# Experts by token: indirect transfers to seats of 128 rows in place of all experts on all tokens

## The chip, the cores and the metric

The kernel runs on one core of a Trainium2 chip. The metric is the device time of one execution in microseconds. The profile comes from one profiled execution; its span runs from the first to the last instruction.

## The reference

One transformer layer on x of 2048 tokens by 256, in fp32. First attention with 16 heads of 128 and weights given as codes and scales, then a mixture of eight experts of which each token uses two:

```python
x = x + layernorm(attention(layernorm(x)))
z = layernorm(x)
probs = softmax(z @ Wr)                      # 8 experts
topk_w, topk_idx = top_k(probs, 2)
topk_w = topk_w / topk_w.sum(-1)
combine = (topk_w * one_hot(topk_idx, 8)).sum(k)
h = silu(z @ Wg[e]) * (z @ Wu[e])            # every e: 256 -> 176
out = sum_e combine[:, e] * (h @ Wd[e])      # 176 -> 256
x = x + layernorm(out)
```

## The kernel before, in words

Five engines run programs written by hand, in written order, and hand over through semaphores: SyncE (`block.sync`) issues all DMAs, GpSimd (`block.gpsimd`), TensorE (`block.tensor`), ScalarE (`block.scalar`), VectorE (`block.vector`). For precision every factor of a product is split in a high and a low part (`_hi`, `_lo`, fp32r), and `product3` (L497 to L499) makes three matmuls of each product.

Attention runs over 128 blocks (16 heads by 8 blocks of 256 rows). SyncE's loop `for n in range(HALVES)` (L318) issues some weight loads of the next head and then `turn_blocks(n)` (L307), 16 transfers of 128 KB that turn the probabilities (L316); it waits first until GpSimd's `pT_lo` (L409) has freed the buffer (L193). The change leaves this part as it is but for what it adds to SyncE's loop and ahead of GpSimd's.

The expert stage begins once `acc` holds the sum over the heads. `pre(c, s)` handles a chunk of 512 tokens in eleven small steps: first normalization of `acc` (L1002), residual on GpSimd (L466), moments (L989), second normalization, transposes (L686) to `xT_hi` (L934) and `xT_lo`, logits for the eight experts (sixteen matmuls of 16 and 8 columns, L696 and L699), exponentials, rank (L1253 to L1264), and `comb`, the two weights of each token, transposed and split. `PRE_AT` (L236) says in which step each part stands.

The matmuls run in 44 steps, 4 chunks by 11 groups of 128 of the 1408 hidden columns of all eight experts. A step makes gate and up (`gate_up`, 12 matmuls of 512 columns into `ps_s`), spreads the tokens' weights over the hidden columns with one matmul (`expand_comb`, L735), takes silu on ScalarE (L961), two products on VectorE (L1312, L1316), the split (L967 on ScalarE, L478 on GpSimd), and `down` two steps later (12 matmuls of 256 columns, L749 to L752), which sums all experts in `ps_a`. So every token goes through all eight experts, and a weight of zero takes six of them out. The splits of the weights (`split_hi` L918 and L923, `split_lo`) stand between the steps of the first chunk. `hooks` puts the next chunk's `pre` and the last chunk's `post` (moments, normalization, residual L473, store) between the steps, so three of the four chunks are routed beside matmuls.

```python
for n in range(STEPS + LAG):
    if n < STEPS:
        gate_up(n)
        expand_comb(n)
    if n >= LAG:
        down(n - LAG)
    hooks(n, pre, post)
```

## Time and profile before

| | us |
|---|---|
| median of 3 runs | 2115.59 (2112.35 to 2116.29) |
| span of the profiled execution | 2115.3 |
| TensorE busy in the span | 2049.6 (97%), 13236 matmuls |
| VectorE, ScalarE, GpSimd busy | 1730.4, 1410.8, 1548.8 |
| mean granted TensorE clock | 0.986 |

The page gives no total of its own for the profiled execution beside its span; the median of the runs is 0.3 us above the span. Matmuls are pipelined and a busy TensorE counts their overlap once, so the distance between two starts is what a matmul costs, and its own duration is longer. A granted clock of 1.00 is 2.4 GHz and 0.50 is 1.2 GHz.

### The profile page before, as it was taken

Reading aid. Unit: us, or ns where it says so; the run is one execution under the profiler, and the core shown is the slowest. Engines: PE = TensorE matmul, PEld = TensorE weight load, DVE = VectorE, ACT = ScalarE, POOL = GpSimd, SP = SyncE. Lnnn points to the kernel's source line nnn. Section 1 sums busy time; section 2 is a strip of 40 time slices with the busy share of each in tenths; the row PEclk is TensorE's granted clock in tenths of the full one; section 3 lists DMA queues with packets and bytes.
Section 4 is the critical chain, followed back from the end, with each engine's and each line's share of the span. In section 5 each row is a group of like instructions: output and inputs, shape, how many; then the busy total and the mean of one; then the engine's idle time right before and its main releaser. Section 6 shows DMA issues by size and latency. Waiting matters only on the chain.

```text
span 2115.3 us, 36713 instructions
## 1 busy us (share of the span) xinstructions
PE 2049.6 (97%) x13236; PEld 1866.8 (88%) x13236; DVE 1730.4 (82%) x2523; ACT 1410.8 (67%) x2575; POOL 1548.8 (73%) x1329
## 2 busy tenths in 40 slices
PE   7999999999999999999999999999999999949998
PEld 5899999999999999999999999899989999838887
DVE  6888878988989888988888898888888888865553
ACT  5777767776777667776677677766777677625343
POOL 2679778886879777877797787877787678846333
PEclk9999999999999999999999999999999999969999
DMA  4667657776667666766676666766676567740000
GB/s 99 155 156 178 158 139 163 170 164 158 146 160 175 151 149 153 181 155 140 162 174 161 148 155 155 179 147 150 153 170 154 136 161 165 161 121 1 11 11 21
DMA packets 216599, 298.50 MB, mean 141 GB/s; under 512 B 44897, under 2 KB 85345, under 8 KB 216417
## 3 DMA queue, kind: packets, MB, share of 16 engines
q1 hardware_dynamic: 216416, 296.15, 59.8%
q8 instruction: 105, 1.72, 0.4%
q14 instruction: 78, 0.63, 0.1%
HBM read 25.46 MB, written 2.10 MB: 13 GB/s over the span
## 4 chain that ended last, share of the span: by engine, by line
PE 84%; SPq 5%; POOL 3%; DVE 3%; ACT 2%; DMA 1%; issue 1%; POOLq 0%; DVEq 0%; ACTq 0%
PE ps_s L497 14%; PE ps_s L498 14%; PE ps_s L499 14%; PE ps_a L499 12%; PE ps_a L498 12%; PE ps_a L497 12%; SPq L316 4%; POOL pT_lo L409 3%; ACT probs L819 1%; PE ps_a L749 1%; PE ps_a L752 1%; PE ps_a L751 1%; DMA pT<-probs 1%; DVE part_max L1065 1%; PE ps_s L735 0%
## 5 line engine op out<-in xcount | busy, mean ns | idle before, releaser
L409 POOL TENSOR_TENSOR pT_lo<-pT,pT_hi 128x512 fp32r<-128x512 f32 x1024 | 1302.8, 1302 | 358.6 <-ACT pT_hi L832 357.6
L832 ACT ACTIVATE pT_hi<-pT 128x512 fp32r<-128x512 f32 x1024 | 612.4, 628 | 232.6 <-DMA pT<-probs 163.5
L819 ACT ACTIVATE probs<-ps_s,shift 128x1024 f32<-128x1024 f32 x512 | 566.6, 1109 | 223.3 <-DVE shift L1074 223.0
L1065 DVE TENSOR_REDUCE part_max<-ps_s 128x1 f32<-128x1024 f32 x512 | 622.0, 1217 | 67.5 <-PE ps_s L499 65.8
L1084 DVE STREAM_TRANSPOSE probs<-probs 128x1024 f32<-128x1024 f32 x512 | 619.4, 1229 | 65.4 <-ACT probs L819 64.6
L497 PE MATMUL ps_a<-pT_hi,v_hi 128*128 128x256 f32 x2048 | 578.7, 283 | 1.5 <-POOL pT_lo L409 1.4
L499 PE MATMUL ps_a<-pT_hi,v_lo 128*128 128x256 f32 x2048 | 579.9, 283 | 0.0
L498 PE MATMUL ps_a<-pT_lo,v_hi 128*128 128x256 f32 x2048 | 579.7, 283 | 0.0
L497 PE MATMUL ps_s<-kT_hi,qT_hi 128*128 128x512 f32 x1024 | 405.2, 396 | 11.7 <-ACT probs L819 8.5
L497 PEld LDWEIGHTS ps_a<-pT_hi,v_hi 128*128 128x128 f32 x2048 | 391.8, 191 | 19.0 <-POOL pT_lo L409 2.5
L498 PEld LDWEIGHTS ps_a<-pT_lo,v_hi 128*128 128x128 f32 x2048 | 391.8, 191 | 15.5
L498 PE MATMUL ps_s<-kT_lo,qT_hi 128*128 128x512 f32 x1024 | 403.9, 394 | 0.0
L499 PE MATMUL ps_s<-kT_hi,qT_lo 128*128 128x512 f32 x1024 | 399.2, 390 | 0.0
L499 PEld LDWEIGHTS ps_a<-pT_hi,v_lo 128*128 128x128 f32 x2048 | 391.8, 191 | 0.0
L499 PEld LDWEIGHTS ps_s<-kT_hi,qT_lo 128*128 128x128 f32 x1024 | 192.4, 188 | 43.7
L497 PEld LDWEIGHTS ps_s<-kT_hi,qT_hi 128*128 128x128 f32 x1024 | 193.9, 189 | 39.4 <-ACT probs L819 10.4
L498 PEld LDWEIGHTS ps_s<-kT_lo,qT_hi 128*128 128x128 f32 x1024 | 193.8, 189 | 21.5
L478 POOL TENSOR_TENSOR h_lo<-hid,h_hi 128x512 fp32r<-128x512 f32 x44 | 57.0, 1295 | 100.3 <-ACT h_hi L967 100.1
L1127 DVE SCALAR_TENSOR_TENSOR acc<-ps_a,rinv,acc 128x256 f32<-128x256 f32 x240 | 104.1, 475 | 6.1 <-PE ps_a L499 5.9
L819 ACT ACTIVATION_READ_ACCUMULATOR probs<-ps_s,shift 128x1 f32 x512 | 99.0, 193 | 0.0
L1312 DVE TENSOR_TENSOR hid<-silu_g,ps_s 128x512 f32<-128x512 f32 x44 | 30.2, 687 | 77.4 <-PE ps_s L499 68.0
L961 ACT ACTIVATE silu_g<-ps_s 128x512 f32<-128x512 f32 x44 | 26.3, 599 | 89.5 <-PE ps_s L499 89.4
(160 smaller groups left out, 2917.5 us busy)
## 6 DMA issues: line engine op xcount, KB each, us to landing
pT<-probs SPq DMA_DIRECT2D x2048, 128.0 KB, 2.5
pT<-in_L_attn_x SPq DMA_DIRECT2D x4, 512.0 KB, 5.7
codes<-in_L_attn_wk_codes SPq DMA_DIRECT2D x16, 128.0 KB, 2.4
scales<-in_L_attn_wk_scales SPq DMA_DIRECT2D x64, 32.0 KB, 3.0
codes<-in_L_attn_wo_codes SPq DMA_DIRECT2D x16, 128.0 KB, 2.3
scales<-in_L_attn_wo_scales SPq DMA_DIRECT2D x64, 32.0 KB, 1.9
x<-in_L_attn_x SPq DMA_DIRECT2D x4, 512.0 KB, 7.1
layer_out<-x SPq DMA_DIRECT2D x8, 256.0 KB, 2.1
```

Source lines behind the costliest of these rows:

```text
L316: sp.dma_start(dst, src[:, :, b, :]).then_inc(pT_loaded[s % 2], 16)
L409: pool.tensor_tensor(pT_lo[:, p, :].rearrange("p (i n) -> p i n", i=Q4), pT[:, s % 2, g, :, t:t + 2, :].rearrange("p i t q -> p i (t q)"), ...
L478: pool.tensor_tensor(h_lo[:, n % HRING, :], hid[:, n % 2, :], full(h_hi[:, n % HRING, :]), ALU.subtract)\
L497: nc.tensor.matmul(dst, lhs_hi, rhs_hi, start=first, stop=False)
L498: nc.tensor.matmul(dst, lhs_hi, rhs_lo, start=False, stop=False)
L499: return nc.tensor.matmul(dst, lhs_lo, rhs_hi, start=False, stop=last)
L819: nc.scalar.activation(out, src, ACT.Exp, bias=shift[:, s % SLOTS, r:r + 1], scale=SCALE, accum_out=sums[:, s % SLOTS, r, g:g + 1])\
L832: nc.scalar.activation(pT_hi[:, p, :].rearrange("p (i n) -> p i n", i=Q4), pT[:, s % 2, g, :, t:t + 2, :].rearrange("p i t q -> p i (t q)" ...
L1065: V.tensor_reduce(part_max[:, s % SLOTS, r, g:g + 1], ring_of("s", w, NG2 * r + g), AX.X, ALU.max)\
L1084: V.transpose(tile, tile).then_inc(sm["p_turned"], 1)
L1127: ins = V.scalar_tensor_tensor(acc[:, t, :], part, scale, acc[:, t, :], ALU.mult, ALU.add)
L1312: V.tensor_tensor(hid[:, n % 2, :], silu_g[:, n % 2, :], ps_bank(b), ALU.mult)\
```

## The change

The 16 tiles of 128 tokens form two parts of eight, routed in three runs (tiles 0 to 3, 4 to 7, 8 to 15). A part has 23 seats of 128 rows, enough for any routing: each expert gets as many whole seats as its tokens need. Matmuls with a triangle of ones and with ones count each token's place, VectorE works out for each token two row numbers and for each seat its expert, and GpSimd sends each tile's normalized rows twice by indirect transfer to `x_rows` in HBM. SyncE loads a seat, TensorE transposes it, reads the seat's expert number into a register and multiplies with that expert's weights alone: the rows are now the stationary operand and the weights, 352 and 256 columns, the moving one. Results are stored to `y_rows`, and GpSimd fetches two rows for each token, which are weighed and added. The rows of `x_rows` are cleared during attention, since a seat may be part empty. All weights are split before the first seat. The three parts of the stage (routing of part 0, of part 1, the seats) stand in written order on each engine. The core of the diff:

```diff
-    G = E * I // P
-    STEPS = NCH * G
+    KD = I // 2
+    RUNS = [(0, 4), (4, 4), (8, 8)]
+    PART_TILES = [(0, 8), (8, 8)]
+    SEATS = [2 * n + E - 1 for _, n in PART_TILES]
+    NS = sum(SEATS)
+    XR = 4
+    GR = 4
+    YS = 4
+    GO = SEATS[0] + 8
 @block.sync
                 turn_blocks(n)
+                if NH <= n < NH + NS:
+                    sp.dma_start(x_rows[u][seat * P:(seat + 1) * P, :], zeros[:, :]).then_inc(x_cleared, 16)
...
+            for n in range(NS + 9):
+                if n < NS:
+                    load_seat(n)
+                if n >= 9:
+                    store_seat(n - 9)
 @block.gpsimd
+            def send(r):
+                if r == 0:
+                    pool.wait_ge(x_cleared, 16 * NS)
+                pool.wait_ge(sm["row_done"], r + 1)
+                for t in tiles_of(r):
+                    pool.wait_ge(sm["xn2_done"], t + 1)
+                    for k in range(2):
+                        pool.indirect_dma_start(x_rows[PART_OF_RUN[r]][:, :], bass.IndirectOffsetOnAxis(row[:, t, k:k + 1], 0),
+                                                acc[:, t, :], None).then_inc(x_sent[PART_OF_RUN[r]], 16)
+            def fetch(t):
+                u = part_of_tile(t)
+                if t == PART_TILES[u][0]:
+                    pool.wait_ge(sm["gu_lo_done"], E)
+                    for b in range(YS):
+                        pool.wait_ge(y_stored[b], 16 * len(range(b, FIRST_SEAT[u] + SEATS[u], YS)))
+                wait(pool, "ysum_done", t - GR + 1)
+                for k in range(2):
+                    pool.indirect_dma_start(yg[:, t % GR, k, :], None, y_rows[u][:, :],
+                                            bass.IndirectOffsetOnAxis(row[:, t, k:k + 1], 0))\
+                        .then_inc(yg_loaded[t % GR], 16)
-            pre_all(pool, pre)
-            prepare_pick()
...
+            residual(0)
+            residual(1)
+            for e in range(E):
+                gate_up_lo(e)
+            send(0)
+            send(1)
+            residual(2)
+            for e in range(E):
+                down_lo(e)
+            send(2)
+            for t in range(PART_TILES[0][1]):
+                fetch(t)
+            for t in range(PART_TILES[0][1]):
+                add_residual(t)
+            for t in range(PART_TILES[0][1], TT):
+                fetch(t)
+            for t in range(PART_TILES[0][1], TT):
+                add_residual(t)
 @block.tensor
+            def gate_up(j):
+                if n == 0:
+                    pe.wait_ge(sm["expert_ready"], u + 1)
+                if j == 0:
+                    pe.wait_ge(sm["gu_lo_done"], E)
+                expert_at[j] = pe.value_load(expert_i[0:1, u, n:n + 1], min_val=0, max_val=E - 1)
+                wait(pe, "xs_lo_done", j + 1)
+                wait(pe, "h_done", j - 1)
+                for c in range(DC):
+                    hi, lo = xs_hi[:, j % 2, c * P:(c + 1) * P], xs_lo[:, j % 2, c * P:(c + 1) * P]
+                    w_h, w_l = (gu_both[:, c, b, bass.ds(expert_at[j], 1), :].rearrange("p a n -> p (a n)")
+                                for b in range(2))
+                    last = product3(ps_gate(j), hi, lo, w_h, w_l, first=c == 0, last=c == DC - 1)
+            def down(j):
+                pe.wait_ge(sm["hs_lo_done"], j + 1)
+                wait(pe, "y_copied", j)
+                for k in range(2):
+                    hi, lo = hs_hi[0:KD, j % 3, k * P:(k + 1) * P], hs_lo[0:KD, j % 3, k * P:(k + 1) * P]
+                    w_h, w_l = (d_both[0:KD, k, b, bass.ds(expert_at[j], 1), :].rearrange("p a n -> p (a n)")
+                                for b in range(2))
+                    last = product3(ps_y, hi, lo, w_h, w_l, first=k == 0, last=k == 1)
+            turn_rows(0)
+            route(0)
+            turn_rows(1)
+            route(1)
+            count_all(0)
+            count_places(0)
+            count_places(1)
+            turn_rows(2)
+            route(2)
+            turn_rows(3)
+            route(3)
+            turn_x(0)
+            for n in range(NS + 3):
+                turn_h(n - 2)
+                turn_x(n + 1)
+                gate_up(n)
...
+                down(n - 3)
 @block.scalar
+            for n in range(NS + 4):
+                hidden_hi(n - 2)
+                seat_hi(n + 1)
+                seat_out(n - 4)
+                gate(n)
+                if GO <= n < GO + PART_TILES[0][1]:
+                    weigh(n - GO)
 @block.vector
+            sum_logits(2)
+            rows_lo(3)
+            sum_logits(3)
+            shift_logits(2)
+            seat_lo(0)
+            for n in range(NS + 4):
+                hidden_lo(n - 2)
+                seat_lo(n + 1)
+                hidden(n)
+                if n == 0:
+                    choose(2)
+                if n == 1:
+                    seat_starts(1)
...
+            for t in range(PART_TILES[0][1], TT):
+                combine(t)
+            out_scale(1)
```

## Rows read from the trace of the kernel before

**Rows 1.** The page's part 4: the chain that ended last, shares by engine.

```profile
PE 84%; SPq 5%; POOL 3%; DVE 3%; ACT 2%; DMA 1%; issue 1%; POOLq 0%; DVEq 0%; ACTq 0%
```

**Rows 2.** Stretches: busy us per engine, TensorE's granted clock, DMA share, GB/s.

```profile
1880.00:1900.00 20.00, 10.18 (x37) 8.29 (x38) 8.88 (x18) 5.37 (x8) 3.21 (x4) 0.50 0.00 1
1900.00:1920.00 20.00, 20.00 (x104) 16.99 (x103) 13.80 (x27) 10.90 (x21) 17.90 (x18) 0.98 0.00 0
```

**Rows 3.** Timeline of VectorE and TensorE, 1870 to 1897: start us, duration us, engine, line.

```profile
1870.27 0.74 DVE L1002 TENSOR_SCALAR acc<-acc,mv,rstd 128x256 f32<-128x256 f32 x2
...
1882.68 1.11 PE L686 MATMUL ps_s<-ident,acc 128*128 128x128 f32 x4 [17.78 <-DVE acc L1002]
...
1887.83 0.35 PE L696 MATMUL ps_s<-wr_both,xT_hi 128*128 128x16 f32 x1 [1.50 <-DVE xT_lo L1236]
...
1891.02 0.35 PE L699 MATMUL ps_s<-wr_both,xT_lo 128*128 128x8 f32 x1
...
1896.26 0.77 PE L497 MATMUL ps_s<-xT_hi,gu_hi 128*128 128x512 f32 x1
```

**Rows 4.** Groups by form, 1850 to 2116: count, busy us, mean ns, idle before.

```profile
L478 POOL TENSOR_TENSOR h_lo<-hid,h_hi 128x512 fp32r<-128x512 f32 x44 | 57.0, 1295 | 100.3 <-ACT h_hi L967 100.1
...
L1312 DVE TENSOR_TENSOR hid<-silu_g,ps_s 128x512 f32<-128x512 f32 x44 | 30.2, 687 | 77.4 <-PE ps_s L499 68.0 <-ACT silu_g L961 7.5 <-issue 1.9
...
L961 ACT ACT_TABLE_LOAD x8 | 10.3, 1283 | 0.1
...
L1002 DVE TENSOR_SCALAR acc<-acc,mv,rstd 128x256 f32<-128x256 f32 x16 | 8.6, 545 | 0.0
...
L918 ACT ACTIVATE gu_hi<-gu_raw 128x512 fp32r<-128x512 f32 x11 | 6.8, 621 | 0.0
L989 DVE BATCH_NORM_STATS2 stats<-x 128x6 f32<-128x256 f32 x16 | 6.7, 419 | 0.9 <-POOL x L466 0.9
...
L923 ACT ACTIVATE d_hi<-d_raw 128x256 fp32r<-128x256 f32 x11 | 4.5, 405 | 0.0
...
L1256 DVE TENSOR_TENSOR ties<-ties,before 128x256 f32<-128x256 f32 x4 | 1.7, 426 | 0.1
...
L1270 DVE TENSOR_REDUCE wsum<-comb 128x4 f32<-128x32 f32 x4 | 0.7, 186 | 0.1
```

**Rows 5.** Timeline of TensorE's matmuls on the warm clock, 1951 to 1986.

```profile
1951.14 0.39 PE L735 MATMUL ps_s<-combT,pick 128*128 128x512 f32 x1
1951.37 0.28 PE L749 MATMUL ps_a<-d_hi,h_hi 128*128 128x256 f32 x1
1951.48 0.28 PE L751 MATMUL ps_a<-d_lo,h_hi 128*128 128x256 f32 x1
...
1985.10 0.25 PE L699 MATMUL ps_s<-wr_both,xT_lo 128*128 128x8 f32 x1
1985.21 0.26 PE L696 MATMUL ps_s<-wr_both,xT_hi 128*128 128x16 f32 x1
```

**Rows 6.** Chain in order of time, SyncE's issues near 1838: start us, us, what.

```profile
1838.19 0.59 SPq L316
...
1838.83 0.60 SPq L316
```

**Rows 7.** Timeline of SyncE after attention: its longest issue.

```profile
1853.89 2.09 SPq L303 DMA_DIRECT2D gu_raw<-in_L_ffn_Wg  x1
```

**Rows 8.** DMA issues by line: count, KB each, median us to landing.

```profile
layer_out<-x SPq DMA_DIRECT2D x8, 256.0 KB, 2.1
```

**Rows 9.** Waits, 100 to 1800 us: total us, times, longest; SyncE's, TensorE's largest.

```profile
SPq L193 <- POOL pT_lo L409: 244.1, 90, 9.0
...
PEld ps_s L497 <- ACT probs L819: 5.0, 5, 2.2
```

**Rows 10.** Timeline of the tail: TensorE's last matmul, GpSimd's residual additions.

```profile
2105.42 0.28 PE L752 MATMUL ps_a<-d_hi,h_lo 128*128 128x256 f32 x1
...
2109.77 2.96 POOL L473 TENSOR_TENSOR x<-x,y_sb 128x256 f32<-128x256 f32 x4 [5.82 <-DVE y_sb L1303]
```

More of the change, by code:

```diff
@@ new lines, in sandwich_layer @@
+        weight = sb("weight", [P, TT, 2], f32)
+        wsum = sb("wsum", [P, TT], f32)
+        fills = sb("fills", [P, E, YR], f32)
+        held = sb("held", [P, E], f32)
+        seats = sb("seats", [P, E], f32)
+        upto = sb("upto", [P, E, E], f32)
+        until = sb("until", [P, E], f32)
+        first_row = sb("first_row", [P, E], f32)
+        passed = sb("passed", [P, max(SEATS), E], f32)
+        expert = sb("expert", [P, max(SEATS)], f32)
+        expert_i = sb("expert_i", [P, PARTS, max(SEATS)], mybir.dt.int32)
@@ new lines, in weigh, with out_std @@
+            def weigh(t):
+                act.wait_ge(yg_loaded[t % GR], 32 * (t // GR + 1))
+                act.wait_ge(sm["weight_ready"], 1 + max(r for r in range(len(RUNS)) if RUNS[r][0] <= t))
+                wait(act, "out_ready", t - YR + 1)
+                nc.scalar.activation(ysum[:, t % YR, :], yg[:, t % GR, 0, :], ACT.Identity, bias=zero[:, 0:1],
+                                     scale=weight[:, t, 0:1]).then_inc(sm["ysc_done"], 1)
+            def out_std(u):
+                act.wait_ge(sm["eps3"], u + 1)
+                nc.scalar.activation(std3[:, :], std3[:, :], ACT.Sqrt).then_inc(sm["std3_done"], 1)
@@ L981, in _ @@
+            for t in range(PART_TILES[0][1], TT):
+                weigh(t)
+            out_std(1)
+            for t in range(PART_TILES[0][1], TT):
+                out_norm(t)
         @block.vector
@@ L1318, in _, with after, first_norm @@
-            pre_all(dve, pre)
-            dve.wait_ge(sm["pick_hi_done"], 1)
-            V.tensor_copy(pick[EP:2 * EP, :], pick[0:EP, :]).then_inc(sm["pick_done"], 1)
-            for n in range(STEPS + LAG):
-                if n < STEPS:
-                    hidden(n)
-                hooks(n, pre, post)
+            steps = itertools.count(1)
+            def after(n):
+                return [next(steps) for _ in range(n)][-1]
+            def first_norm(r):
+                for t in tiles_of(r):
+                    normed(acc, acc, t).then_inc(sm["z_norm"], 1)
@@ new lines, in seat_lo, with hidden @@
+            def seat_lo(j):
+                if not 0 <= j < NS:
+                    return
+                dve.wait_ge(sm["xs_hi_done"], j + 1)
+                V.tensor_tensor(xs_lo[:, j % 2, :], ps_x, full(xs_hi[:, j % 2, :]), ALU.subtract)\
+                    .then_inc(sm["xs_lo_done"], 1)
+            def hidden(j):
+                if not 0 <= j < NS:
+                    return
+                dve.wait_ge(sm["silu_done"], j + 1)
+                wait(dve, "h_t", j - 2)
+                V.tensor_tensor(hid[:, j % 3, :], silu_g[:, j % 2, :], ps_gate(j)[:, I:2 * I], ALU.mult)\
+                    .then_inc(sm["h_done"], 1)
@@ L1327 @@
+            for t in range(PART_TILES[0][1], TT):
+                combine(t)
+            out_scale(1)
 _INS = ["x", "wq_codes", "wq_scales", "bq", "wk_codes", "wk_scales", "bk", "wv_codes", "wv_scales", "bv",
```

781 lines of the change are left out of this document (454 added, 327 removed).

## The prediction

> **What bounds the kernel now.** I read the chain that ended last first: TensorE carries 84% of it [rows 1]. I then cut the span into stretches. Attention is untouched in its arithmetic; behind it stands the stage that the change rewrites. The table of stretches shows it [rows 2]: from 1880 to 1900 TensorE is busy for half the time at clock 0.50, then comes a stretch of 20.00 at clock 0.98, and nine more as full until 2100. The stage lasts from 1870.3 (VectorE's first `acc` normalization) to the last end at 2115.3, 245 us, in three pieces: 26.0 us of routing until the first expert matmul at 1896.26 [rows 3], 44 steps bound by TensorE until its last end at 2105.7, and 9.6 us of tail [rows 10]. I argue against the span, 2115.3; the median of the runs shown is 0.3 above it, which I add at the end. A difference of 0.2% (4.2 us) is about what can be measured on this kernel.
>
> A present step costs, by the distance between starts on the warm clock [rows 5]: 12 matmuls of 512 columns and the spread of the weights (one more) at 0.23, 12 of 256 columns at 0.12: 13 x 0.23 + 12 x 0.12 = 4.4 us; 44 of them are 194 us, and the transposes and logits of the later chunks fill the stretch up to the 209 us seen.
>
> **What the change puts there.** All eight experts on all tokens are 16 x 8 = 128 tile-expert pairs; the change runs a fixed 46 seats (23 for each half of the tokens), whatever the routing gives. Three prices make the sum.
>
> *One seat, s.* TensorE: 6 matmuls of 352 columns, between the 256 and the 512 price [rows 5], so 6 x 0.16 = 0.98; 6 of 256 columns, 6 x 0.12 = 0.71; four transposes, each a weight load and 128 columns, at 0.11 like the pairs of weight load and 16 columns [rows 5]: 0.44. That is 2.14 us. ScalarE has four passes of 176 to 256 columns, at most 0.40 each as the 256-column `d_hi` [rows 4], 1.5 us; VectorE three, at most 0.45 each, 1.3 us. Neither binds, but ScalarE's order couples the step: its copy of seat n-4 stands behind the copy of seat n+1, and `down(n-3)` waits for it. New is the register: one load of the expert's number for each seat, then an address for each of eight weight views. No row shows a register instruction. From below its cost is nothing, if TensorE's queue still holds matmuls while its sequencer works. From above it is a load that stalls once per seat like the longest fixed load in the trace, a table load at 1.28 [rows 4]. The nearest rows are the 16-column pairs that start 0.11 apart warm, so 0.055 for an instruction at most [rows 5]; a dozen register instructions at that price are 0.66. I take s = 2.14 + 0.66 = 2.80, bounds 2.14 and 3.42. 46 x 2.80 = 128.8.
>
> The Trainium skill, "DMA: Bandwidth & Descriptors", section on latency and other measured facts, gives a tensor load a floor of about 600 ns; no run here shows one. By that figure, as an estimate, 46 loads left uncovered would be 28 us beside the register arithmetic; the sum does not use it.
>
> *One indirect transfer, c.* There are 64, each moving 128 rows of 1 KB, all issued by GpSimd. The trace has none. The nearest rows are plain issues of 128 KB on SP, 0.64 apart [rows 6]; the longest issue that SP shows here is 2.09 [rows 7]. GpSimd takes 1.295 for a form for which VectorE takes 0.687, 1.9 times as long [rows 4]; 0.64 x 1.9 = 1.2. I take 1.2, bounds 0.6 and 2.1. What counts is how many lie on the path: 16 before the first seat (the first half's rows) and 16 after the last one (the second half's results). The other 32 lie beside seats: the second half's sends have 23 seats, 64 us, for 19 us of work, and the first half's fetches are used from step 31 on.
>
> *The way to the first seat.* From 1870.3, on the cold clock:
> - first half's norms: 8 passes at 0.545, four moments at 0.55 (0.42 for the statistics, then a short aggregation), scale 1.2: 7.8; ScalarE's norms of four tiles 1.6, then the second four's moments, split of two experts (0.62 for 512 columns, so 0.85 each) and norms: 5.7 more [rows 4].
> - two groups one after the other through TensorE: transposes 1.1 for four, copies 0.6 and 0.7, sixteen logit matmuls 3.4 (first start 1887.83, last end 1891.37) [rows 3, 4]: 5.3 for the first, 7.3 for the second, whose transposes stand behind the first's logits on TensorE.
> - exponential and choice, on VectorE five operations on 256 columns at 0.43, six small ones at 0.19, the exponential and its hand-overs: 4.0; counts, seat starts, places, rows: 3.5 [rows 4].
> Together 33.6. The eight splits of gate and up weights on GpSimd (8 x 1.30 x 704/512 = 14.3) lie under this; GpSimd is done with them near 1891.
> - sixteen sends: 16 x 1.2 = 19.2. GpSimd's residual of the second half stands behind them.
> - then, by the written order, TensorE's first seat stands behind `route(3)` and VectorE's `seat_lo(0)` behind the logits of the second half: residual 8 x 0.74 = 5.9, moments and scale 1.8, norms of four tiles 1.6, two groups through TensorE 2.8 + 0.7 + 3.4 + 2.2 + 0.6 + 0.7 + 3.4 = 13.8, logits 0.9, exponential with a table load 1.5, first seat's copies 0.9: 26.4 [rows 3, 4, 10]. The loads of the seats lie beside it.
> - some 30 hand-overs between engines at 0.2 each: 6.0.
>
> Then in the first steps VectorE also chooses for the second half: five operations on 512 columns at 0.69, two small ones, and a chain through TensorE for the seat starts, less the slack it has in a step (2.8 - 1.3): 5.0 too long in all.
>
> *The way out.* Last hidden tile through silu, transposes, down and copy 3.3; store to memory 2.3, by the 2.1 of the output's [rows 8]; 16 fetches 19.2; landing 2.2; weigh, add, moments 1.8; scale 1.2; norm 0.4; eight residual additions on GpSimd 5.9 (now four in 2.96 [rows 10]); last stores 2.8 [rows 8]. 39.1, against 9.6 now.
>
> *Attention.* SP gains 46 issues that clear rows, 28 us of queue time, one for each of 46 blocks. SP waits 244 us in 90 places for GpSimd's `pT_lo` between 100 and 1800, and the largest wait that TensorE shows there is 5 us for ScalarE [rows 9]; five weight issues in one block already pass without a hole. I cost it at nothing; were the cover gone, up to 28 us.
>
> **Sum.** 1870.3 + 33.6 + 19.2 + 26.4 + 6.0 + 5.0 + 128.8 + 39.1 = 2128.4, with 0.3 outside the span 2129. In short 1961.5 + 32c + 46s: the matmul stretch loses 81 us (209 to 129) and the two ends gain 94.
>
> **The rivals.**
> - *The register work is covered* (faster). Matmuls and weight loads wait in TensorE's queue, and a seat is bound by 2.14 plus a small wait for `seat_out`: s = 2.3, total 1961.5 + 38.4 + 105.8 = 2106; with c = 0.9, 2096. For it: TensorE today shows no hole between instructions of different lines [rows 5]. Against it: the load comes between waits, so the sequencer may not be far ahead. It decides from s below about 2.5. Chance 0.37.
> - *The load stalls the sequencer.* s = 2.14 + 1.28 = 3.42: 1961.5 + 38.4 + 157.3 = 2157. The sequencer can't compute addresses before the number has arrived. Chance 0.13.
> - *The indirect transfers are slow.* c = 2.1: 1961.5 + 67.2 + 128.8 = 2158. Chance 0.08. The place is GpSimd ahead of its residual and after the last store.
> - *The clock stays low.* The clock granted from 1880 to 1900 is 0.50, with TensorE busy for half the time [rows 2]. At half the clock a seat is at least 6 x 0.29 + 6 x 0.21 + 4 x 0.28 = 4.1 us (the transposes by [rows 3]), total 2189. A seat at half the clock fills TensorE, though, and when it was filled after 1896 the clock rose: chance 0.03.
> The page "TensorE: Matmul & The Clock Gate", Part 1 of the Trainium skill, says that sustained work brings the clock back; the trace agrees (0.50, then 0.98).
> - *It doesn't do what it says*: the seat count is fixed, so no routing makes it cheaper or dearer. No chance is set aside.
>
> **How the numbers follow.** The forecast, s between 2.55 and 3.1 with c between 0.9 and 1.6, has 0.39, and a tenth of all lies within 0.2% of no change, at its lower edge. Faster by over 0.2% takes the covered case and a little of the lower edge: 0.38. Slower takes the rest: 0.52. Cases of both signs hold most of the chance; the forecast's own range is 2108 to 2155. The whole range, down through the covered case at c near 0.6 and up past the two slow cases, is 2080 to 2168.
>
> **What would show it.** In the profile after: the first gate matmul near 1956, not 1896; distance between seats 2.8 (2.3 or 3.4 decide for a rival); 16 GpSimd issues 19 us long ahead of the second half's residual, and 16 more between the last store of a seat and the last norm; TensorE's last matmul near 2092; the first `acc` normalization still at 1870, with stretches of 20.00 for TensorE before it. The forecast is wrong if seats start before 1945, if the seat distance is under 2.5, or if attention has grown by more than 5 us.

## The result and the profile after

The kernel after takes 2135.46 us, the median of 4 runs (2133.17 to 2136.89), the kernel before 2115.03 (4 runs, 2112.35 to 2116.29): ratio 1.0093, 95% interval 1.008 to 1.0105. It is slower by 0.9%. The profiled execution took 2136.37 us with a span of 2134.5.

First the chain that ended last, from the page of the kernel after, shares of the span by engine:

```profile
PE 70%; SPq 10%; POOL 7%; DVE 5%; ACT 4%; issue 3%; DMA 2%; POOLq 0%; ACTq 0%; DVEq 0%
```

TensorE carried 84% [rows 1] and carries 70% now; GpSimd went from 3% to 7%, and SyncE's queue (SPq) from 5% to 10%. The same change shows in the stretches of the kernel after (columns as in [rows 2]):

```profile
1880.00:1900.00 20.00, 7.34 (x32) 6.57 (x32) 11.48 (x30) 9.48 (x19) 14.67 (x11) 0.50 0.07 21
...
1920.00:1940.00 20.00, 0.00 (x0) 0.00 (x0) 3.73 (x13) 0.00 (x0) 13.76 (x18) 0.50 0.27 92
1940.00:1960.00 20.00, 5.00 (x23) 4.60 (x23) 13.60 (x19) 5.21 (x11) 10.33 (x9) 0.50 0.00 0
1960.00:1980.00 20.00, 14.03 (x56) 11.88 (x57) 9.73 (x27) 6.45 (x12) 0.00 (x0) 0.59 0.09 26
1980.00:2000.00 20.00, 18.88 (x127) 17.42 (x127) 10.86 (x35) 8.85 (x28) 9.69 (x11) 0.94 0.45 142
2000.00:2020.00 20.00, 19.06 (x131) 17.10 (x129) 8.74 (x25) 9.97 (x32) 5.69 (x6) 1.00 0.48 154
2100.00:2120.00 20.00, 0.00 (x0) 0.00 (x0) 6.56 (x18) 3.60 (x6) 14.38 (x15) 0.50 0.47 144
```

Where TensorE had a full stretch from 1900 on, it now has nothing from 1920 to 1940 and nothing again after 2100. Both empty stretches belong mostly to GpSimd's indirect transfers. Here is GpSimd's timeline before the first seat, kernel after:

```profile
1911.41 1.19 POOL L547 DMA_INDIRECT x_rows<-acc,row  x1 [14.52 <-issue]
1912.91 0.96 POOL L547 DMA_INDIRECT x_rows<-acc,row  x1 [0.31 <-issue]
...
1922.23 0.97 POOL L547 DMA_INDIRECT x_rows<-acc,row  x1 [2.03 <-issue]
...
1932.83 0.97 POOL L547 DMA_INDIRECT x_rows<-acc,row  x1 [2.04 <-issue]
...
1935.09 5.48 POOL L525 TENSOR_TENSOR x<-x,acc 128x256 f32<-128x256 f32 x8
1940.54 9.79 POOL L536 TENSOR_TENSOR d_both<-d_raw,d_both 88x512 fp32r<-88x512 f32 x8
```

A send is 0.96 us of GpSimd (the first one 1.19) and starts 1.27 after the one before it, except that after every seventh there is a gap of 2.03 in place of 0.30. Sixteen take 23.7 us. Then comes the residual, then eight splits of the down weights. What VectorE does beside those splits is the largest surprise (timeline of VectorE, kernel after):

```profile
1940.60 0.43 DVE L1202 BATCH_NORM_STATS2 stats<-x 128x6 f32<-128x256 f32 x1
1941.06 0.18 DVE L1204 BATCH_NORM_AGGREGATE mv<-stats 128x2 f32<-128x6 f32 x1
1941.28 9.08 DVE L1449 TENSOR_SCALAR std<-mv 128x8 f32<-128x8 f32 x1
1950.63 0.20 DVE L1451 RECIPROCAL rstd<-std 128x8 f32<-128x8 f32 x1 [0.27 <-ACT std L1077]
```

An operation on 8 columns takes 9.08 us and ends at 1950.36, when GpSimd's splits end (1950.33). The two operations ahead of it (0.43 and 0.18) were not held, though GpSimd's run had begun at 1940.54. The whole routing of the second half stands behind `std`.

The next view is a seat on the warm clock, in TensorE's timeline of the kernel after (gate and up L592 to L594 from `xs`, down from `hs`, the pairs of transposes L868 and L837):

```profile
2010.57 0.42 PE L592 MATMUL ps_a<-gu_both,xs_hi 128*128 x1
2010.83 0.33 PE L593 MATMUL ps_a<-gu_both,xs_hi 128*128 x1
2010.99 0.32 PE L594 MATMUL ps_a<-gu_both,xs_lo 128*128 x1
...
2011.63 0.29 PE L592 MATMUL ps_s<-d_both,hs_hi 88*128 x1
...
2012.35 0.39 PE L868 MATMUL ps_s<-ident,hid 128*88 128x128 f32 x2
2012.57 0.38 PE L837 MATMUL ps_s<-ident,xg 128*128 128x128 f32 x2
2013.03 0.42 PE L592 MATMUL ps_a<-gu_both,xs_hi 128*128 x1
```

The prices of the columns hold: 0.16 for 352, 0.12 for 256, 0.11 for a transpose. Two distances are longer: 0.26 from the first gate matmul to the second, and 0.46 from the second pair of transposes to the next seat. The kernel of run 2, which has no registers, tells them apart:

```profile
2000.70 0.38 PE L837 MATMUL ps_s<-ident,xg 128*128 128x128 f32 x2
2000.84 0.41 PE L592 MATMUL ps_a<-gu_both,xs_hi 128*128 128x352 f32 x1
2001.09 0.32 PE L593 MATMUL ps_a<-gu_both,xs_hi 128*128 128x352 f32 x1
```

There the pair of transposes costs 0.14, so its 0.46 is where the registers show (part of that comes back at the seat's down); the first matmul costs 0.25 there as well, so that is not theirs. The 46 gate starts run from 1970.39 to 2090.49, 120.1 us: the first five distances sum to 17.5, the two around ScalarE's table loads (2075 to 2079) to 6.75, the other 38 are 2.52 each.

The tail, from the chain in order of time of the kernel after (`gu_raw` is the buffer into which GpSimd fetches):

```profile
2098.38 0.39 ACT y_sb L1130
2098.79 1.74 DMA y_rows<-y_sb
2100.64 0.71 issue
2101.36 0.96 POOL gu_raw L559
...
2120.36 2.70 DMA gu_raw<-y_rows,row
2123.08 0.61 ACT gu_raw L1137
```

### The profile page after: what moved, and what is told of

Its sections match the earlier page's. It is cut to its first block, busy times and chain, and to the rows that moved or that the text cites. A ratio compares the mean times of both kernels' runs of the same rounds, so it can differ in the third digit from the quotient of the medians.

```text
span 2134.5 us, 37062 instructions
## 1 busy us (share of the span) xinstructions
PE 1977.1 (93%) x12882; PEld 1805.4 (85%) x12882; DVE 1726.7 (81%) x2582; ACT 1422.3 (67%) x2687; POOL 1548.3 (73%) x1345
## 4 chain that ended last, share of the span: by engine, by line
PE 70%; SPq 10%; POOL 7%; DVE 5%; ACT 4%; issue 3%; DMA 2%; POOLq 0%; ACTq 0%; DVEq 0%
PE ps_s L592 12%; PE ps_a L592 12%; PE ps_s L593 11%; PE ps_s L594 11%; PE ps_a L594 11%; PE ps_a L593 11%; SPq L360 8%; POOL pT_lo L484 4%; ACT probs L966 2%; DMA pT<-probs 1%; DVE part_max L1278 1%; POOL x_rows L547 1%; POOL gu_raw L559 1%; ACT pT_hi L979 1%; DVE probs L1297 1%
## 5 line engine op out<-in xcount | busy, mean ns | idle before, releaser
L592 PE MATMUL ps_a<-pT_hi,v_hi 128*128 128x256 f32 x2048 | 578.9, 283 | 3.2 <-POOL pT_lo L484 3.1
L594 PE MATMUL ps_a<-pT_hi,v_lo 128*128 128x256 f32 x2048 | 580.0, 283 | 0.0
L592 PE MATMUL ps_s<-kT_hi,qT_hi 128*128 128x512 f32 x1024 | 406.0, 397 | 14.2 <-ACT probs L966 11.1
L592 PEld LDWEIGHTS ps_a<-pT_hi,v_hi 128*128 128x128 f32 x2048 | 391.6, 191 | 21.0 <-POOL pT_lo L484 2.9
L594 PE MATMUL ps_s<-kT_hi,qT_lo 128*128 128x512 f32 x1024 | 400.0, 391 | 0.0
L594 PEld LDWEIGHTS ps_a<-pT_hi,v_lo 128*128 128x128 f32 x2048 | 391.7, 191 | 0.0
L592 PEld LDWEIGHTS ps_s<-kT_hi,qT_hi 128*128 128x128 f32 x1024 | 194.1, 190 | 42.5 <-ACT probs L966 13.5
L594 PEld LDWEIGHTS ps_s<-kT_hi,qT_lo 128*128 128x128 f32 x1024 | 192.9, 188 | 43.7
L593 PEld LDWEIGHTS ps_s<-kT_lo,qT_hi 128*128 128x128 f32 x1024 | 194.1, 190 | 21.5
L592 PE MATMUL ps_a<-w_o_hi,oT_hi 128*128 128x256 f32 x256 | 72.4, 283 | 7.3 <-DVE oT_lo L1305 7.3
L547 POOL DMA_INDIRECT x_rows<-acc,row x32 | 31.0, 968 | 66.2 <-DVE row L1547 34.8
L1355 DVE SCALAR_TENSOR_TENSOR kT_lo<-ps_s,bias_k,kT_hi 128x1024 fp32r<-128x1024 f32 x32 | 41.1, 1284 | 44.1 <-ACT kT_hi L1009 44.1
```

Of the source, the lines that this page charges most:

```text
L547: pool.indirect_dma_start(x_rows[PART_OF_RUN[r]][:, :], bass.IndirectOffsetOnAxis(row[:, t, k:k + 1], 0), acc[:, t, :], None).then_inc(x_s ...
L592: nc.tensor.matmul(dst, lhs_hi, rhs_hi, start=first, stop=False)
L593: nc.tensor.matmul(dst, lhs_hi, rhs_lo, start=False, stop=False)
L594: return nc.tensor.matmul(dst, lhs_lo, rhs_hi, start=False, stop=last)
L1355: V.scalar_tensor_tensor(kT_lo[:, cols], ring_of("k", h, b), bias_all["k"][:, h:h + 1], full(kT_hi[:, cols]), ALU.add, ALU.subtract).then_ ...
```

## The experiments

Twelve kernels were run, each beside the kernel before; the ratios are to that kernel, whose median stayed between 2114.6 and 2115.7 us. Differences in us between two kernels are differences of their medians. The runs try two theories against each other: that the three prices of the prediction (registers, transfers, the way to the first seat) carry the result, or that waits between engines that it did not price do.

**1. The clears alone.** The kernel before with the 46 transfers of zeros in attention, with what they need (GpSimd sets a buffer of zeros ahead of attention and waits for the transfers behind it), and nothing else of the change:

```diff
+                if NH <= n < NH + NS:
...
+                    seat = n - NH
+                    sp.dma_start(x_rows[seat * P:(seat + 1) * P, :], zeros[:, :]).then_inc(x_cleared, 16)
```

> The kernel before with the change's 46 clearing stores of 128 KB after 46 of the 128 attention blocks, and nothing else of the change. Theory (the clears delay attention): in the changed kernel the first acc normalization starts 4.9 us later than before, and the shift grows from head 1 to head 7, where the clears are, to 7 us. Then this kernel loses 4 to 8 us, its first acc normalization starts near 1875 to 1878, and the expert stage is as long as before. Rival (the shift is drift from one execution to another, or GpSimd's constants): within 2 us of the kernel before.

Measured: 2119.12 us, ratio 1.0013 (1.0004 to 1.0023). SyncE's and TensorE's largest waits from 120 to 1870, of this kernel:

```profile
PE ps_s L509 <- ACT probs L831: 7.3, 6, 1.8
PE ps_a L509 <- DVE oT_lo L1104: 7.1, 4, 3.2
...
SPq L198 <- POOL pT_lo L419: 224.1, 86, 8.4
```

In the same window the kernel before has 4.0, 7.0 and 247.0 for them. The queue's slack fell by 23 us and covered most of the 46 issues, but VectorE's first `acc` normalization moved from 1870.27 to 1875.14, and the expert stage behind it stayed as long (244.6 against 245.0 us). By the ratio the loss is 1 to 5 us, at or below the lower end of the 4 to 8 expected. One execution against one says little here, but attention is the same in all fourteen kernels, except for the clears and constants set ahead of it: in the eight profiles with them the first normalization starts at 1872.4 to 1875.3 (mean 1874.0), in the six without at 1868.1 to 1871.6 (mean 1869.5). So "covered" was a statement on the sum of the slack, not on each of the 46 places; which of them delayed attention was not looked at.

**2. No registers.** The kernel after with the expert fixed at build:

```diff
-                expert_at[j] = pe.value_load(expert_i[0:1, u, n:n + 1], min_val=0, max_val=E - 1)
+                expert_at[j] = j % E
```

> The changed kernel with the expert of seat j fixed as j mod 8 at build time: no register load and no register in an address. It computes with the wrong experts. Everything else, the 46 seats among it, stays. Theory (most of the register work lies beside the matmuls; what is left is the wait ahead of a seat's first matmuls): the distance between seats falls from 2.46 to about 2.2, 46 x 0.25 = 11 us off. Rival A (the register work is fully covered, 2.46 comes from ScalarE's order): less than 3 us off. Rival B (it costs what the forecast took, 0.66): 25 to 30 us off, but then the seat would come out at 1.8, less than the matmuls' own 2.14.

Measured: 2122.84, ratio 1.0033 (1.0022 to 1.0043), 12.6 under the kernel after. Behind the first four distances its seats are 2.27 apart almost without exception, and TensorE's stretches from 1980 to 2060 are 20.00. The seat's price without registers, summed to 2.14 beforehand, is 2.27; registers add 0.25, not 0.66. Theory held: 11 us off was expected, near 2.2 for the seat.

**3. The load without the arithmetic.** One run parts the two halves of that 0.25:

```diff
-                expert_at[j] = pe.value_load(expert_i[0:1, u, n:n + 1], min_val=0, max_val=E - 1)
+                pe.value_load(expert_i[0:1, u, n:n + 1], min_val=0, max_val=E - 1)
+                expert_at[j] = j % E
```

> The kernel after, in which TensorE still loads each seat's expert number into a register but addresses the weights of expert j mod 8, fixed at build: only the address arithmetic is gone. It leaves out the choice of the right expert, so its output is not the reference's. The seat distance was 2.52 us with load and arithmetic, 2.27 with neither. If the load is what costs (a stall of the sequencer, once a seat), the distance stays near 2.5 and the time near that of the kernel after, 2135. If the arithmetic on eight views is what costs, the distance falls to 2.27 to 2.3 and the time comes to 2123, as with fixed experts. Theory: arithmetic, about 2124; anything between splits the 12.6 us by the same share.

Measured: 2125.93, ratio 1.0049 (1.0036 to 1.0062). TensorE's loads of gate weights by form, 1970 to 2100, idle before them at the end of each line; first this kernel:

```profile
L592 PEld LDWEIGHTS ps_a<-gu_both,xs_hi 128*128 128x128 f32 x89 | 17.4, 196 | 3.1 <-issue 2.8
```

and the kernel after:

```profile
L592 PEld LDWEIGHTS ps_a<-gu_both,xs_hi 128*128 128x128 f32 x92 | 18.1, 197 | 16.3 <-issue 15.9
```

Without registers that idle time is 0.0. From the first to the last gate matmul it is 108.5 us without registers, 111.9 with the load alone, 120.1 with both: 3.4 for 46 loads, 8.2 for the arithmetic. An average of 0.07 us for a load hides where it falls. Over the 27 distances behind the first five, seats are 2.27 apart without registers, 2.27 with the load alone and 2.52 with both, so in steady seats the load costs nothing and the arithmetic the whole 0.25. The load's 3.4 us lie in the first five distances (17.9 against 15.9) and in the eight distances behind the 32nd (2.47 each against 2.28); why there was not tried. The rival "the load stalls the sequencer" has fallen. The Trainium skill, "DMA: Bandwidth & Descriptors", section on latency and other measured facts, has a floor of about 600 ns for such a load; whatever its latency here, the steady seats show all of it covered.

**4. The down splits ahead of the sends.** The wait of 9.08 us, taken away by order alone, on GpSimd and on ScalarE:

```diff
             for e in range(E):
+                down_lo(e)
             send(0)
             send(1)
             residual(2)
-            for e in range(E):
-                down_lo(e)
```

> The changed kernel with the eight down-weight splits of GpSimd moved from behind residual(2) to ahead of send(0), where GpSimd is idle for 14.5 us, and ScalarE's eight halves moved ahead of rows_hi(1). Theory (VectorE's tiny tensor_scalar std, 9.08 us long in the changed kernel, stands for GpSimd's uninterrupted run of additions on the port the two share): that instruction falls to about 0.2 us, the first seat starts 9 us earlier, the whole loses 8 to 9 us. Rival (the long std has another cause, or the way to the first seat has another limit of equal length): the std stays at 9 us or the time moves by less than 3 us.

Measured: 2128.22, ratio 1.0054 (1.0034 to 1.0074), 7.2 less. VectorE's row of the same operation, in this kernel's timeline:

```profile
1944.59 0.17 DVE L1449 TENSOR_SCALAR std<-mv 128x8 f32<-128x8 f32 x1
```

9.08 became 0.17, and what changed beside it is GpSimd's work. ScalarE's splits moved too, but in the kernel after ScalarE stood idle from 1910.6 to 1950.39, so nothing of its own lay beside `std` there. In the profiled executions the first gate matmul comes 5.6 earlier (1964.79 for 1970.39), not the 9 expected. The other 3.4 went where the splits now lie, beside the first half's choice: three passes that took 0.42 take 1.37 to 1.49 there, and the first send moves from 1911.41 to 1914.76.

**5. The second half's routing beside the sends.** On top of 4, `residual(2)` before the sends and VectorE's `first_norm(2)` before the first half's logits:

```diff
+            residual(2)
             send(0)
             send(1)
-            residual(2)
...
+            first_norm(2)
             sum_logits(0)
...
-            first_norm(2)
```

> As e3, and also GpSimd's residual(2) ahead of send(0) and VectorE's first_norm(2) ahead of sum_logits(0), so that the second half is routed while GpSimd issues the first half's sends. Theory (the first seat is late because the written order puts the second half's residual behind 16 sends and the seats behind the second half's logits): the first gate matmul starts near 1941 instead of 1970, bound by the last send and a seat's load; the whole loses 25 to 31 us against the changed kernel and ends at 2105 to 2110, 5 to 10 us under the kernel before. Rival (the routing of the second half slows the sends or the sends slow it, by the port that VectorE and GpSimd share): under 15 us off.

Measured: 2113.92, ratio 0.9993 (0.9982 to 1.0003), 21.5 less than the kernel after: the serial order was the dearest thing in the change. The promised 25 were not reached. First gate matmul: 1949.45, not 1941. The second half's norm on VectorE ran beside GpSimd's splits at four times what it takes in the kernel after, where GpSimd only issues sends beside it. First this kernel's timeline, then that of the kernel after:

```profile
1893.67 11.16 DVE L1215 TENSOR_SCALAR acc<-acc,mv,rstd 128x256 f32<-128x256 f32 x8
1913.50 2.72 DVE L1215 TENSOR_SCALAR acc<-acc,mv,rstd 128x256 f32<-128x256 f32 x8
```

The same eight passes take 5.12 us in the kernel after where GpSimd's residual stands beside them (first half, 1875.21). In this kernel the first send moved from 1911.4 to 1919.4.

**6. The clears after attention.** The same 46 issues, in a loop of their own ahead of the seats' loads:

```diff
-                if NH <= n < NH + NS:
-                    ...
+            for j in range(NS):
+                sp.dma_start(x_rows[u][seat * P:(seat + 1) * P, :], zeros[:, :]).then_inc(x_cleared, 16)
```

> The changed kernel with the 46 clearing stores moved out of the attention blocks to SyncE's queue behind the weight loads, where SyncE waits some 45 us for the first half's sends. Theory (the clears in attention cost it some 4 us, as adding them to the kernel before did: ratio 1.0013): 3 to 5 us off, the first acc normalization back near 1871. Rival (the stores now collide with something on the way to the first send, x_cleared coming late): no gain or a loss, and the first send waits for x_cleared past 1911.

Measured: 2130.66, ratio 1.0071 (1.0054 to 1.0087), 4.8 less; the first send comes at 1904.58 and does not wait for them. The way from the first `acc` normalization to the first send is 36.2 us in both kernels. With run 1 this puts the clears' price in attention at 3 to 5 us, and shows none behind it.

**7. Twice the scratch for descriptors.**

```diff
-    nc = bacc.Bacc("TRN2", target_bir_lowering=False, num_devices=1, dynamic_dma_scratch_size=1024)
+    nc = bacc.Bacc("TRN2", target_bir_lowering=False, num_devices=1, dynamic_dma_scratch_size=2048)
```

> The changed kernel with twice the scratch for software DMA descriptors (2048 for 1024). In the changed kernel the sends start 1.27 us apart, but after every seventh there is a gap of 2.0 us. Theory (the descriptor ring holds seven transfers of 128 rows, and GpSimd waits for it to empty): the first gap moves to behind the fourteenth send, the sixteen sends take 21.5 to 22 instead of 23.7 us, the whole loses about 2 us. Rival (the gaps come from something else that recurs): gaps stay after each seventh, no change.

Measured: 2133.14, ratio 1.0083 (1.0067 to 1.01). GpSimd's timeline of this kernel has one gap, after the fourteenth send:

```profile
1926.79 0.96 POOL L547 DMA_INDIRECT x_rows<-acc,row  x1 [0.30 <-issue]
1929.86 0.97 POOL L547 DMA_INDIRECT x_rows<-acc,row  x1 [2.12 <-issue]
```

With 1024 the gap comes after every seventh send of either half, with 2048 after the fourteenth, so it goes with the scratch. That the scratch runs full there is the plain reading, but not shown to the end: 16 fetches in a row ran at 1024 without a gap. Sixteen sends take 22.0 instead of 23.7; the time's 2.3 us lie within the two intervals.

**8. Half the sends.** The first half's second-choice rows are not sent, and SyncE waits for half as many before it loads the first seat:

```diff
-                    for k in range(2):
+                    for k in range(1 if PART_OF_RUN[r] == 0 else 2):
```

> The changed kernel without the second choice's sends of the first half: 8 sends in place of 16 before the first seat. Rows of half the pairs stay zero there. Theory (each send lies on the path to the first seat, through the residual of the second half that stands behind them): 8 x 1.27 and one gap of 1.8, 11 to 13 us off; the first gate matmul near 1958. Rival (something else, such as the second half's norms, would bound the first seat anyway): under 5 us off.

Measured: 2122.56, ratio 1.0033 (1.0019 to 1.0046), 12.9 less. Eight issues and one gap are 8 x 1.27 + 1.73 = 11.9, and from the first `acc` normalization to the first gate matmul this kernel takes 83.3 us for 95.2, 11.9 less. So the sends lie on the path with their whole length.

**9. All of it together.** Down splits early (on GpSimd six ahead of the sends, two behind; on ScalarE all ahead of the second group of transposed rows), `residual(2)` ahead of them, the second half's first norm on ScalarE, clears after attention, scratch 2048:

```diff
+            residual(2)
+            for e in range(E - 2):
+                down_lo(e)
             send(0)
             send(1)
-            residual(2)
-            for e in range(E):
+            for e in range(E - 2, E):
                 down_lo(e)
...
+            for t in range(8, 16):
+                nc.scalar.activation(acc[:, t, :], acc[:, t, :], ACT.Identity, bias=shifted[:, t:t + 1],
+                                     scale=rstd[:, t:t + 1]).then_inc(sm["z_norm2"], 1)
```

> e3 and e5 and e6 together, GpSimd's residual(2) ahead of send(0), and the second half's first normalization given to ScalarE, where VectorE shared a port with GpSimd and took 8 us longer for it in e4. Two of the eight down splits stay behind the sends. Theory (three waits: the clears 4, the second half's routing behind the sends 30, VectorE's wait on GpSimd 9, partly the same time): first send near 1908 to 1912, first gate matmul near 1938, total 2098 to 2106, 10 to 17 us under the kernel before. Rival (the sends are put off by what is moved ahead of them, as in e4): 2110 or more.

Measured: 2107.2, ratio 0.9962 (0.9948 to 0.9976), faster than both kernels, though 1 us outside the 2098 to 2106 expected. The first send (1909.28) and the first gate matmul (1937.58) came where expected. Its VectorE timeline shows the choice beside GpSimd's splits, which end at 1903.5:

```profile
1901.26 1.16 DVE L1501 TENSOR_TENSOR beats<-ex 128x256 f32<-128x256 f32 x1 [0.30 <-ACT ex L1102]
1902.35 1.48 DVE L1502 TENSOR_TENSOR ties<-ex 128x256 f32<-128x256 f32 x1
1903.86 0.43 DVE L1504 TENSOR_TENSOR ties<-ties,before 128x256 f32<-128x256 f32 x1
```

**10. All splits behind the sends.** On top of 9:

```diff
             residual(2)
-            for e in range(E - 2):
-                down_lo(e)
             send(0)
             send(1)
-            for e in range(E - 2, E):
+            for e in range(E):
                 down_lo(e)
```

> The combined kernel (2107.2 us) with all eight GpSimd splits of the down weights behind the first half's sends, none ahead of them. In the combined kernel VectorE's choice passes took 0.94 to 1.48 us beside GpSimd's split run and 0.42 after it. If that contention is real, they take 0.42 to 0.5 each, the first send comes about 5 us earlier (near 1904 instead of 1909.3), and the time is 2102 to 2104. The splits then end some 10 us after the last send, near 1936, before the first down matmul. Rival: the passes are slow for another reason, or the second half's logits behind the same splits lose what the first half gains: 2107.

Measured: 2108.53, ratio 0.9962 (0.9949 to 0.9975): no gain. The first half did gain: with the splits gone from beside it, VectorE's second set of choice passes takes 0.42 each, and from the first `acc` normalization to the first send it is 36.5 us for 41.2. The wait came back in the second half (VectorE's timeline of this kernel):

```profile
1932.27 7.73 DVE L1486 TENSOR_TENSOR ex<-logits,lmax 128x64 f32<-128x64 f32 x1
```

and GpSimd's:

```profile
1930.12 9.80 POOL L539 TENSOR_TENSOR d_both<-d_raw,d_both 88x512 fp32r<-88x512 f32 x8
```

So it is not a matter of the form TENSOR_SCALAR: this is a TENSOR_TENSOR on 64 columns, and it too ends with GpSimd's run, at 1940.0 against 1939.9. The reduction ahead of it, which reads PSUM, took 0.22 at 1931.76. From the first send to the first gate matmul it was 28.3 us in kernel 9 and is 34.2 here. The stated rival held.

**11. Filling TensorE's idle stretches.** On top of 10, transposes of the identity that nothing reads:

```diff
             count_places(1)
+            keep_warm(70)
             turn_rows(2)
+            keep_warm(14)
             route(2)
             turn_rows(3)
+            keep_warm(10)
             route(3)
+            keep_warm(14)
             turn_x(0)
```

> The kernel with all splits behind the sends, and 108 transposes of the identity into an unused piece of PSUM in TensorE's idle stretches between the first half's counts and the first seat (70, 14, 10, 14). The granted clock was 0.50 there and the first five seats took 4.9 us more than five later ones. If TensorE is kept busy and the clock rises to 1.00, the second half's logits take half of 3.4 us twice and the first seats 2.5 each: 5 to 8 us less than without the transposes, near 2096. If the clock stays at 0.50, the added transposes delay the routing where they overrun their gaps: 0 to 6 us more than without them, 2103 to 2109.

Measured: 2102.29, ratio 0.994 (0.9926 to 0.9953), the fastest of all. The stretches of kernel 11 (columns as above):

```profile
1900.00:1920.00 20.00, 15.97 (x114) 15.56 (x114) 13.20 (x56) 6.09 (x12) 10.82 (x12) 0.76 0.19 67
...
1920.00:1940.00 20.00, 11.97 (x76) 10.20 (x75) 6.36 (x13) 5.69 (x10) 14.61 (x13) 0.74 0.26 86
```

The granted clock is 0.76 and 0.74 where kernel 10 has 0.50 twice. VectorE waits 2.04 for the second half's logits instead of 3.67, twice. That puts `ex` (1926.04) ahead of GpSimd's splits (1927.83), and the wait of 7.73 is gone. From the first `acc` normalization to the first gate matmul it is 64.7 us for 70.6, which is the gain; how much of it is the clock alone and how much the wait that it avoids, one run can't part. The seats themselves gained nothing: after an idle 3.8 us for `xg` the first one starts at the cold spacing, and the first five distances sum to 18.6.

**12. Transposes up to the seat.** On top of 11:

```diff
-            keep_warm(14)
+            keep_warm(34)
             turn_x(0)
+            keep_warm(8)
```

> The kernel with transposes in the idle stretches, with 34 instead of 14 of them ahead of the first seat's own transposes and 8 behind those, so that TensorE has work up to the first gate matmul. With 14 it idled 3.8 us there, its first seat ran at the cold spacing (0.29 between gate matmuls, against 0.16), and the first five distances summed to 18.6 us. If the idle 3.8 us are what costs the clock, the first gate matmuls are 0.16 apart and the five distances sum to 16 or less: 2 to 3 us less, 2099 to 2101. If the early seats are slow for VectorE's choice for the second half and for ScalarE's table load (the second distance alone was 6.48), the sum stays near 18 and the time near 2102; where the transposes overrun, up to 1 us more.

Measured: 2144.03, ratio 1.0138 (1.0113 to 1.0162), 42 us more than 11 and outside every number stated. TensorE's timeline of this kernel:

```profile
1917.30 0.27 PE L612 MATMUL ps_a<-ident 128*128 128x128 f32 x1 [0.95 <-issue]
...
1919.44 0.33 PE L784 MATMUL ps_s<-ident,acc 128*128 128x128 f32 x1 [1.14 <-issue]
...
1940.60 6.26 PE L612 MATMUL ps_a<-ident 128*128 128x128 f32 x34
...
1977.42 0.57 PE L595 MATMUL ps_s<-d_both,hs_hi 88*128 x1 [7.03 <-issue]
```

On the question asked, the first two seats do run at the warm spacing, 0.16 between gate matmuls, so keeping TensorE busy up to them was enough for that. But the second distance is 5.09 all the same, since TensorE then waits 3.10 for VectorE's choice, and the next seats are at 0.29 again. The five distances sum to 17.8: the second branch of the expectation.

The 42 us come from holes: in the profiled executions the first gate matmul is 15.1 us later than in kernel 11, and the seats take 147.0 instead of 120.9 from first to last. TensorE issues single transposes a microsecond apart from 1916 to 1926, waiting for nothing that the profile shows, and stands still from 1970.4 to 1977.42, from 1981.7 to 1988.37 and from 2045.2 to 2050.03. It is not TensorE alone. In the same places ScalarE stands, put down to a release that the profile can't name (`remote`); its timeline in this kernel has:

```profile
1974.39 0.38 ACT L1134 ACTIVATE hs_hi<-ps_s 88x256 fp32r<-88x256 f32 x1 [5.39 <-remote]
1984.28 0.32 ACT L1126 ACTIVATE silu_g<-ps_a 128x176 f32<-128x176 f32 x1 [7.11 <-remote]
```

TensorE's hole of 7.03 ends 0.24 us after ScalarE's next copy of a result (1976.80 to 1977.18), for which `down` waits by the program. No other kernel has such `remote` waits. Each time GpSimd is issuing indirect transfers: sends to 1927.85 and from 1964.35 to 1986.2, fetches from 2039.8 to 2049.6. Where the holes begin TensorE's program is still that of kernel 11, which has none there, its eight transposes taking 1.04 us in one run.

One thing in the traces points at the instructions themselves. The profile records transfers of a queue named `q8 instruction`. From 1905 to 1927 kernel 11 has one and this kernel none; its next one starts at 1927.85, when the last send ends. From 1961 to 1988 kernels 10 and 11 have two each and this kernel none; the next one is at 1989.36. That instructions arrive late while GpSimd issues is thus a guess that fits. It is not shown, and why 28 transposes further on bring it about is open.

## Why the prediction was right

The call was 2129 us and slower; measured was 2135.5, slower. Against the span it is 2128.4 to 2134.5, 6.1 us, and it was right partly because errors cancelled: attention was 4.9 over, the way to the first gate matmul 10.0 over, and all from there to the end 8.8 under (164.1 for 172.9).

- **Attention at nothing**: 4.9. The term failed as a matter of principle, not of size: slack summed over 1700 us says little of 46 single places. Runs 1 and 6 and the fourteen profiles put it at 3 to 5.
- **The way to the first gate matmul**, predicted as 85.2 from the first `acc` normalization (33.6 + 19.2 + 26.4 + 6.0): 95.2. Of it the sends are 23.7 against 19.2. Their price of 1.2 measured 1.27, and its derivation (SyncE's issue times the 1.9 by which GpSimd is slower at a subtraction) rests on rows of other kinds of work: that it came so near is luck. The rest is two gaps of 1.73 over an ordinary one, which nothing before could show. The remaining 71.5 (66.0 predicted) hold the 9.08 of VectorE's `std`. Without its 8.9 too many the small rows and the hand-over allowance come to 62.6, 3.4 under. The step that failed is the line on the second half's "moments and scale 1.8": from the residual's end (1940.57) to ScalarE's first norm (1951.07) it was 10.5. A clue stood in the trace of the kernel before, in VectorE's timeline beside GpSimd's work:

```profile
1875.03 1.41 DVE L1227 TENSOR_SCALAR std<-mv 128x4 f32<-128x4 f32 x1
1876.92 5.70 DVE L1002 TENSOR_SCALAR acc<-x,mv,rstd 128x256 f32<-128x256 f32 x4
```

  The same `std` takes 0.17 where nothing stands beside it, and a pass of the norm 0.34 where GpSimd only sends, against 1.41 and 1.43 here. The prediction priced the pass by its mean of 0.545 over all places [rows 4], and had no term for what GpSimd does beside it.
- **The seat, s**: 2.80 predicted, 2.52 measured on the warm clock. The bounds held, the forecast's own range (2.55 to 3.1) did not, and 2.52 is just above the point from which the covered rival would decide ("below about 2.5"). The register term was mis-sized: 0.25 for 0.66. A dozen instructions at 0.055, the price of a matmul or weight load, was too much for what stays uncovered; by run 3 it is the address arithmetic that does. The passes without registers were 2.27 for 2.14, 0.1 of it at the first gate matmul.
- **The early excess**: 4.9 in the first five seats against 5.0, but from more causes than named: VectorE's choice, as predicted, and the first gate matmuls at 0.29 instead of 0.16. That 4.9 and 5.0 agree is luck in part. Two table loads in the loop add 1.7, which was not in the sum.
- **The way out**: from the last seat's copy 35.7 against 35.8 (39.1 less the 3.3 of that tile). The pipeline's drain before it was 8.3 from the last gate start, against 6.1.
- **Outside the span**: 1.9 against 0.3. This is no part of the change: every run of the kernel before that was taken with its own span has 1.7 to 1.8 between span and time as well. The 0.3 had the span of one execution set against the median of others.

By the prediction's own formula with the measured prices, 1961.5 + 32 x 1.27 + 46 x 2.52 = 2118.1. That is 0.1% over the kernel before, no change that could be told. Without the two waits that it did not foresee (attention 4.9, `std` 8.9) the kernel would have come to about 2121.7, 0.3% slower, and near the edge. So the sign rests in good part on waits that the prediction did not have. The clock was low for the first seats only; the rival in which it stays low did not come. The forecast's own signs of error read: seats start at 1970, not before 1945; the distance is 2.52, just not under 2.5; attention grew by 4.9, just not over 5.

Experiments 4, 5 and 9 show the larger reason. From the first gate matmul to the last copy the seats take 128 us where the steps took 209. The span still grew by 19, so the rest of the stage and attention grew by 100. Of those 28 come back by the order of the work, the place of the clears and the scratch (21.5 by order alone), and then the two-expert form beats the kernel before by 0.4%, with TensorE kept busy by 0.6%.

## What to carry to other kernels

Leaving out 64% of the expert work (46 of 128 seats) gained 81 us of matmul time and lost 100 around it, since sorting rows is a serial chain through every engine with TensorE idle: price that chain first, and ask what of the second part can run beside the transfers of the first. When GpSimd runs a block of two-operand work back to back, look at every VectorE operation beside it that a chain stands behind. The cure here was order, and moving the block could also move the wait (run 10). Slack summed over a stretch does not cover issues that fall at single places in it.

## What the runs showed of the hardware that was not expected

- **VectorE beside GpSimd.** Two small VectorE operations on SBUF were held until an uninterrupted run of GpSimd's two-operand instructions ended: `std` 9.08 for 0.17, `ex` 7.73 for 0.23. Eight passes of the norm took 11.16 beside such a run, 5.12 beside the residual and 2.72 beside sends. Statistics on SBUF (0.43) and a reduction from PSUM (0.22) were not held. The Trainium skill, "SBUF — State Buffer", section on who interferes with whom, tells of a port pair that the two share and that one instruction holds to its end; the runs agree that the loser waits, and differ in how long: the six to eight instructions of GpSimd that were left of its run, not one. In other places the wait was about one GpSimd instruction or less: the first half's `std`, in the kernel after, took 0.74 and 1.11 while GpSimd's splits ran on, and in kernel 9 choice passes took 1.16 and 1.48. What decides between the two is open.
- **Indirect transfers.** 128 rows of 1 KB cost GpSimd 0.96 us and 0.30 to the next; they took 2.4 us to land as sends and 2.9 as fetches. The sends stop for some 2 us after every 7 (scratch 1024) or 14 (2048); the 16 fetches of the tail ran without such a gap, and why is open.
- **Registers on TensorE.** In steady seats the load of a number costs nothing and the addresses of eight weight views 0.25 us a seat (2.27, 2.27 and 2.52 apart in run 2, run 3 and the kernel after). Over all 46 seats the load adds 3.4 us, 0.07 each on average.
- **The clock.** In the kernel after the granted clock was 0.50 from 1880 to 1960, with TensorE busy 0 to 7.3 us of each 20. Transposes in the idle stretches brought 0.76 and 0.74 (run 11). They paid by the routing that they sped up, not by the seats.
- **Holes in TensorE and ScalarE without a cause in the profile** while indirect transfers are issued (run 12), for 42 us of time; open.
